# Layer 0's shared experts with plain float32 products instead of three products of split operands

## What is computed

```python
def _L0_ffn_ref(x, w_router, wg, wu, wd, sg, su, sd):      # E, TOPK, H, I, NSH = (8, 2, 256, 640, 2)
    logits = jnp.einsum('th,eh->te', xt, w_router)
    topk_w, topk_i = jax.lax.top_k(jax.nn.sigmoid(logits), TOPK)
    ...
    sgate = jax.nn.silu(jnp.einsum('th,jih->tji', xt, sg))
    sup = jnp.einsum('th,jih->tji', xt, su)
    out = out + jnp.einsum('tji,jhi->th', sgate * sup, sd)
x = x + _L0_ffn_ref(_layernorm(x), ...)
```

## Time and profile before

| | |
|---|---|
| median of 3 runs | 1225.46 us (1220.16 to 1228.32) |
| the profiled execution | 1225.15 us |
| its span, first to last instruction | 1223.4 us |
| mean granted clock of TensorE | 0.865 |
| busy: TensorE, VectorE, ScalarE, GpSimd | 965.5, 644.6, 355.5, 242.9 us |

### The profile page before, as it was taken

How to read it: one execution, slowest core, us unless ns; L and a number is a source line. 1 busy time by engine, 2 the same in 40 slices (tenths; PEclk the granted TensorE clock), 3 DMA queues, 4 the chain that set the end, 5 groups by cost and what they waited for, 6 DMA issues and landing times. The chain is left out here.

```text
span 1223.4 us, 13908 instructions
## 1 busy us (share of the span) xinstructions
PE 965.5 (79%) x4883; PEld 625.8 (51%) x4883; DVE 644.6 (53%) x1198; ACT 355.5 (29%) x747; POOL 242.9 (20%) x223
## 2 busy tenths in 40 slices
PE   3666663999998998036878888888887199999997
PEld 1333432786665665013444444444453188888885
DVE  3677675343222222464685666757743555555553
ACT  1222222232222222021523424334332043333332
POOL 0111212300000000602212203213210033344342
PEclk9778775999999999556997797899885599999999
DMA  5000002350578774330000000000000263333201
GB/s 200 1 18 18 18 1 86 100 232 5 180 286 286 274 280 153 113 114 5 3 16 18 1 18 18 1 18 14 1 1 1 91 212 121 97 114 116 94 1 34
DMA packets 36972, 102.68 MB, mean 84 GB/s; under 512 B 4640, under 2 KB 23968, under 8 KB 33712
## 3 DMA queue, kind: packets, MB, share of 16 engines
q1 hardware_dynamic: 35376, 97.70, 23.5%
q0 software_dynamic: 1536, 4.20, 1.0%
HBM read 90.54 MB, written 11.34 MB: 83 GB/s over the span
## 5 line engine op out<-in xcount | busy, mean ns | idle before, releaser
L1286 POOL TENSOR_TENSOR f_h<-f_hu,f_cb 128x512 f32<-128x512 f32 x56 | 92.9, 1659 | 173.3 <-DVE f_hu L1355 173.3
L1114 PE MATMUL ps<-f_rw,f_xT 128*128 128x512 f32 (+1 forms) x276 | 112.8, 532 | 11.2 <-DMA f_rw<-w_routed 10.6
L2028 ACT ACTIVATE b_PX<-ps 128x512 f32<-128x512 f32 x128 | 74.8, 596 | 92.3 <-PE ps L2236 91.3
L1028 DVE TENSOR_TENSOR f_rh<-f_gate,ps 128x256 f32<-128x256 f32 (+1 forms) x69 | 26.0, 377 | 135.8 <-ACT f_gate L974 85.3
L1849 DVE TENSOR_REDUCE b_smax<-ps 128x2 f32<-128x512 f32 x128 | 82.3, 685 | 28.4 <-PE ps L2216 28.2
L1355 DVE TENSOR_TENSOR f_hu<-f_act,ps 128x512 f32<-128x512 f32 x56 | 38.5, 688 | 106.9 <-PE ps L1382 106.9
L1380 PE MATMUL ps<-xh,f_wh 128*128 128x512 f32 x224 | 89.0, 398 | 5.3 <-DVE f_wl L1341 5.3
L1382 PE MATMUL ps<-xh,f_wl 128*128 128x512 f32 x224 | 89.5, 400 | 0.0
L1381 PE MATMUL ps<-xl,f_wh 128*128 128x512 f32 x224 | 89.2, 398 | 0.0
L1310 ACT ACTIVATE f_act<-ps 128x512 f32<-128x512 f32 x56 | 33.6, 601 | 145.7 <-PE ps L1382 145.7
L2236 PE MATMUL ps<-b_Q,b_Cx 100*128 100x256 f32 x256 | 71.8, 381 | 4.6 <-ACT b_Q L2020 3.6
(11 more groups left out here) (288 smaller groups left out, 1914.4 us busy)
## 6 DMA issues: line engine op xcount, KB each, us to landing
f_rw<-w_routed SPq DMA_DIRECT2D x23, 1920.0 KB, 7.9
f_raw<-w_ffn SPq DMA_DIRECT2D x28, 384.0 KB, 4.5
f_cb<-comb SPq DMA_DIRECT2D x16, 512.0 KB, 4.2
f_raw<-w_shared SPq DMA_DIRECT2D x10, 384.0 KB
b_Cx<-ctx_parts SPq DMA_DIRECT2D x96, 32.0 KB
f_cb<-comb SPq DMA_DIRECT2D x8, 384.0 KB, 3.6
rows<-a_empty SPq DMA_DIRECT2D x1, 2944.0 KB, 14.3
f_xs<-rows SPq DMA_DIRECT2D x23, 128.0 KB, 7.5
```

Of the source, the lines that this page charges most:

```text
L1114: mm = nc.tensor.matmul(ps[:, u % 4, 0:2 * n], xT[b % 2][:, c, :], rw[b % R_SLOTS][:, off:off + 2 * n], start=(c == 0), stop=(c == C - 1))
L1286: nc.gpsimd.tensor_tensor(h[u % h_slots][:], hu[u % 2][:], cb[slot][:, t * HT:(t + 1) * HT], ALU.mult).then_inc(h_ready, 1)
L2028: nc.scalar.activation(PX[g % RING][:].rearrange("p c m -> p (c m)"), ps[:, RETS + G_TURN[g] % 2, :], ACT.Exp, scale=XSC).then_inc(turn_re ...
```

## The change

The turned rows are kept once, in float32: `keep_xT` with k = 2 writes straight into a new buffer `XT` [128, 2, 1024], and `route` reads it. `high_part` and `low_part` are gone, `xh` and `xl` serve the layer 1 stages only. In the shared experts every product is one plain float32 matmul of `raw` and `XT` or `h`. The splits of weights and of `h` are gone on both engines, so are the zero products: `start` and `stop` stand on the first and last chunk's products. TensorE waits for the landing of a chunk (`w_loaded`) and for `h_ready`; a weight slot is loaded again, and an `h` slot written again, once `down` is done with it. The order of units on each engine, `LAG` and the numbers of slots stay.

```diff
@@ attention0 @@
-            def low_part(i, s):
-                t = i * 2 + s
-                dve.wait_ge(xh_ready, i * 2 + s + 1)
-                nc.vector.tensor_tensor(xl[:, :, bass.ds(t * P, P)], xT1[s][:], xh[:, :, bass.ds(t * P, P)].bitcast(F32),
-                                        ALU.subtract).then_inc(low_ready, 1)
...
-                to = xT[s] if k == 0 else xT1[s]
-                nc.scalar.copy(to[:], at.rearrange("p (c t) -> p c t", c=C)).then_inc(xT_ready[k], 1)
+                to = (xT[s][:], xT1[s][:], XT[:, :, (i * 2 + s) * P:(i * 2 + s + 1) * P])[k]
+                nc.scalar.copy(to, at.rearrange("p (c t) -> p c t", c=C)).then_inc(xT_ready[k], 1)
...
-            def high_part(i, s):
-                t = i * 2 + s
-                act.wait_ge(xT_ready[2], i * 2 + s + 1)
-                nc.scalar.copy(xh[:, :, bass.ds(t * P, P)], xT1[s][:]).then_inc(xh_ready, 1)
...
@@ routed_experts @@
                 if j >= W_SLOTS:
-                    sp.wait_ge(wh_ready, j - W_SLOTS + 1)
-                    sp.wait_ge(wl_ready, j - W_SLOTS + 1)
+                    sp.wait_ge(down_done, (j - W_SLOTS + 1) * HALVES)
...
-                if u >= 1:
-                    high_h(u - 1)
-                if u % HALVES == 0 and u // HALVES + LEAD < SHARED_CHUNKS:
-                    split(u // HALVES + LEAD)
-            high_h(UNITS - 1)
-            act.wait_ge(sum_done, 1)
+            act.wait_ge(down_done, UNITS)
...
                 if u >= H_SLOTS:
-                    dve.wait_ge(hl_ready, u - H_SLOTS + 1)
+                    dve.wait_ge(down_done, u - H_SLOTS + 1)
                 nc.vector.tensor_tensor(h[u % H_SLOTS][:], act_out[u % 2][:], ps[:, 2 * (u % 2) + 1, :], ALU.mult).then_inc(h_ready, 1)
-                if u >= 1:
-                    low_h(u - 1)
-                if u % HALVES == 1 and u // HALVES + LEAD < SHARED_CHUNKS:
-                    split(u // HALVES + LEAD)
-            low_h(UNITS - 1)
-            dve.wait_ge(sum_done, 1)
+            dve.wait_ge(down_done, UNITS)
...
                 if t == 0:
-                    pe.wait_ge(wh_ready, j + 1)
-                    pe.wait_ge(wl_ready, j + 1)
+                    pe.wait_ge(w_loaded[w], 16 * (j // W_SLOTS + 1))
...
-                        mm = three(ps[:, 2 * (u % 2) + n, :], wh[w][:, at], wl[w][:, at], xh[:, c, tok], xl[:, c, tok],
-                                   c == 0, c == C - 1)
+                        mm = nc.tensor.matmul(ps[:, 2 * (u % 2) + n, :], raw[w][:, at], XT[:, c, tok], start=(c == 0), stop=(c == C - 1))
...
-                pe.wait_ge(hh_ready, u + 1)
-                pe.wait_ge(hl_ready, u + 1)
+                pe.wait_ge(h_ready, u + 1)
...
-                    mm = three(acc[c][t], wh[w][:, at], wl[w][:, at], hh[u % H_SLOTS][:], hl[u % H_SLOTS][:], False, False,
-                               skip_group_check=True)
+                    mm = nc.tensor.matmul(acc[c][t], raw[w][:, at], h[u % H_SLOTS][:], start=(u < HALVES), stop=(u >= UNITS - HALVES),
+                                          skip_group_check=True)
...
-            pe.wait_ge(zeros_set, 1)
-            for c in range(C):
-                for t in range(HALVES):
-
-                    nc.tensor.matmul(acc[c][t], zeros[:, 0:P], zeros[:], start=True, stop=False, skip_group_check=True)
...
-            for c in range(C):
-                for t in range(HALVES):
-                    mm = nc.tensor.matmul(acc[c][t], zeros[:, 0:P], zeros[:], start=False, stop=True, skip_group_check=True)
-            mm.then_inc(sum_done, 1)
```

More of the change, by code:

```diff
@@ L99, in decoder_kernel @@
         with nc.sbuf_tensor("XN", [P, TILES, D], F32) as XN, \
+                nc.sbuf_tensor("XT", [P, C, TOKENS], F32) as XT, \
                 nc.sbuf_tensor("KR", [P, R_ALL], F32) as KR, \
@@ L526, in _ @@
                 for s in range(2):
-                    if last:
-                        low_part(i - 1, s)
-                for s in range(2):
                     if own:
@@ L744, in route @@
                 for c in range(C):
-                    mm = nc.tensor.matmul(side(s)[:, 0:E0], xT1[s][:, c, :], W[:, c, A_R:A_R + E0],
+                    mm = nc.tensor.matmul(side(s)[:, 0:E0], XT[:, c, (i * 2 + s) * P:(i * 2 + s + 1) * P], W[:, c, A_R:A_R + E0],
                                           start=(c == 0), stop=(c == C - 1))
@@ L797, in attention0, with routed_experts @@
     end_program(nc, semaphores)
-def routed_experts(nc, tag, w_shared, w_routed, rows_dram, y_dram, X, XN, xh, xl, K, ps, dest, wk, eb):
+def routed_experts(nc, tag, w_shared, w_routed, rows_dram, y_dram, X, XN, XT, K, ps, dest, wk, eb):
     ctx = ExitStack()
@@ L806, in routed_experts @@
     UNITS = HALVES * SHARED_CHUNKS
-    LEAD, LAG = 2, 2
+    LAG = 2
     W_SLOTS, H_SLOTS = 4, 4
@@ L827, in routed_experts @@
         raw = [sb(f"raw{n}", [P, WC]) for n in range(W_SLOTS)]
-        wh = [sb(f"wh{n}", [P, WC], F32R) for n in range(W_SLOTS)]
-        wl = [sb(f"wl{n}", [P, WC], F32R) for n in range(W_SLOTS)]
         act_out = [sb(f"act{n}", [P, HT]) for n in range(2)]
         h = [sb(f"h{n}", [P, HT]) for n in range(H_SLOTS)]
-        hh = [sb(f"hh{n}", [P, HT], F32R) for n in range(H_SLOTS)]
-        hl = [sb(f"hl{n}", [P, HT], F32R) for n in range(H_SLOTS)]
-        zeros = sb("zeros", [P, HT], BF16)
         oT = [[sb(f"oT{c}{t}", [P, HT]) for t in range(HALVES)] for c in range(C)]
@@ L933, in _ @@
         def _(act):
[L934 to L937, removed]
-                nc.scalar.copy(wh[j % W_SLOTS][:], raw[j % W_SLOTS][:]).then_inc(wh_ready, 1)
-            def high_h(u):
-                act.wait_ge(h_ready, u + 1)
-                if u >= H_SLOTS:
-                    act.wait_ge(down_done, u - H_SLOTS + 1)
-                nc.scalar.copy(hh[u % H_SLOTS][:], h[u % H_SLOTS][:]).then_inc(hh_ready, 1)
-            for j in range(LEAD):
-                split(j)
             for u in range(UNITS):
@@ L981, in _ @@
         def _(dve):
-            def split(j):
-                dve.wait_ge(wh_ready, j + 1)
-                nc.vector.tensor_tensor(wl[j % W_SLOTS][:], raw[j % W_SLOTS][:], wh[j % W_SLOTS][:].bitcast(F32),
-                                        ALU.subtract).then_inc(wl_ready, 1)
-            def low_h(u):
-                dve.wait_ge(hh_ready, u + 1)
-                nc.vector.tensor_tensor(hl[u % H_SLOTS][:], h[u % H_SLOTS][:], hh[u % H_SLOTS][:].bitcast(F32),
-                                        ALU.subtract).then_inc(hl_ready, 1)
-            nc.vector.memset(zeros[:], 0.0).then_inc(zeros_set, 1)
-            for j in range(LEAD):
-                split(j)
             for u in range(UNITS):
@@ L1047, in _ @@
         def _(pe):
-            def three(dst, hi, lo, rhs_hi, rhs_lo, first, last, **kw):
-                nc.tensor.matmul(dst, hi, rhs_hi, start=first, stop=False, **kw)
-                nc.tensor.matmul(dst, hi, rhs_lo, start=False, stop=False, **kw)
-                return nc.tensor.matmul(dst, lo, rhs_hi, start=False, stop=last, **kw)
             def gate_up(u):
```

15 lines of the change are left out of this document (3 added, 12 removed).

## The result

| | before | after |
|---|---|---|
| median of 12 runs | 1225.43 us (1215.22 to 1246.11) | 1237.59 us (1228.08 to 1258.44) |
| ratio after to before | | 1.0095, 95% interval 1.0055 to 1.0136 |

What follows compares the result with a forecast made beforehand. The prediction took TensorE to bound the shared experts. Their stage at +15.4 us, the entry at -2.0 and the attention stage at -0.4 summed to +13.0 us, giving 1238.5 us, range 1232 to 1245.

Steps and rivals of the forecast that it cites:

- Price of a product: Shared experts: a plain float32 product takes 0.858 us against 0.680 for three split matmuls, +21.4 us over 20 units.
- The gap: Shared experts: TensorE's hole from 224.42 to 227.66 us, with the slow matmuls behind it, disappears, -4.8 us.
- The clock at the entry: Start of the shared stage: TensorE's half clock level costs 2.4 us, before and after the change alike.
- The entry: Start of the shared experts: TensorE waits only for chunk 0's landing and starts at about 208.0 instead of 209.97, -2.0 us.
- The attention stage: Attention ahead of the shared experts: removed subtractions free GpSimd's multiply pair, casts give nothing, -0.4 us.
- The new wait on SyncE: Shared weights' reload waits for `down` of both halves; hidden by four units, 20.6 us, so no cost.
- The routed stage: Routed experts behind the shared ones: still 185 us, with their loads there in time.
- The rival of later stages: Everything from 505 us on shifts against what sets the clock, giving a gain: 1233 us; chance 0.10.
- My sign of being wrong: Among the signs that would refute the forecast: a later stage changed by more than 2 us.
- Four single paces: Shared experts' product costs four full single paces, 0.907 us, +5.9 us, 1244.4 in all; chance 0.05.
- A double record: Shared experts' product is one double record of 0.43 us, making the kernel faster, 1187 us; chance 0.03.
- The hole that stays: Shared experts: TensorE's hole stays or comes back elsewhere, +4.8 us, 1243.3 in all; chance 0.12.

Runs made afterwards that it cites:

- before_two_products: The kernel before with the second of the three split products left out (output less exact): 1195.42 us, shared stage 58.6 us.
- after_late_multiply: The changed kernel with eight extra 128x512 multiplies on VectorE ahead of unit 2's multiply: 1251.29 us in one execution, shared stage 106.3 us.
- after_two_slots: The changed kernel with two slots for the shared weights in place of four: 1250.48 us, shared stage 134.0 us.
- the third version: The changed kernel with split products again, except unit 0's gate and up; rows split while first weights load: 1218.29 us, ratio 0.9932 to before.

## Why the prediction was right, and where it was not

- **Price of a product, +21.4.** Right. 5.15 us a unit against 4.08, two records a product, 0.858 us each. It came from L1114 in the same kernel. Nothing of it is hidden, as before_two_products shows from the other side.
- **The gap, -4.8.** Wrong, and the largest miss. The arithmetic of who waits for whom was right: after_late_multiply takes a delay of 4.9 us with no loss, and the late multiply in the profile of after (225.69, 0.9 us late) costs nothing. But I took a feature of one execution for one of the kernel. It came in 2 of the 7 profiles of kernels that split. As the sum was made against the execution that had it, the -4.8 had no counterpart in the median. What made this invisible: the same execution had the least time at the half level in layer 1's attention of the three (189.5 us), and its total lay on the median.
- **The clock at the entry, 2.4.** Mis-sized by 0.6. TensorE starts earlier but the clock doesn't rise earlier by as much: 6.1 us at the half level against 4.8, so 3.0 us lost. With it the stage is 103.0 + 3.0 + 0.3 = 106.3, and the forecast said 105.6.
- **The entry, -2.0.** Right: from load to product 5.1 to 5.3 us before, 3.0 to 3.3 after. That the zero products did nothing for the clock is not shown: no run takes them away alone.
- **The attention stage, -0.4.** Wrong in size: -2.7, of which the slower start of the next stage takes back 1.3. The direct part is about the 0.4 of the working, and it is the subtractions, not the casts. The step that failed is that I stopped there: the table of stretches gave the attention a clock of 0.78, and a small shift on VectorE's side moved how long TensorE stayed at the half level.
- **The new wait on SyncE, 0.** Right; its cover is worth 24.1 us of waits, as after_two_slots shows. **The routed stage** stayed as it was: 183.5 and 184.7 us against 184.3 and 185.3.
- **The sum.** To E: 20.9 - 2.1 - 2.7 = 16.1, and the table says 16. Forecast 13.0, so 3 short. The medians are 12.2 apart, 3.9 less than the stages add up to; without that, some 1241.5 would have been due. That the total lay within 1 us of the forecast is luck. The rival of later stages, a gain of 5 us at the chance of 0.10, fits the 3.9, but the clock's scatter can give as much. My sign of being wrong, a later stage changed by more than 2 us, says little by itself: layer 1's attention was 23 us longer in after's first profile, and differs by 15 between the profiles of before.
- **The rivals.** Four single paces: no, 5.15 and not 5.44 us a unit. A double record: no. The Trainium skill (Perfetto Trace Analysis, Engine Utilization) has the output rate of low/high float32 at half; a whole product has little over a quarter in the trace, since it is two records of 0.43 us against 0.227 us for one matmul of split operands. One record by itself fits the half. The hole that stays: no, it isn't there to begin with.

What stays open is why TensorE's signals come late. It is seen at the multiply of unit 2 or 3 in 4 of the 14 profiles, by 5.5, 6.3, 0.9 and 0.7 us, each time near GpSimd's last indirect transfers, which the ten others have as well. Holding these back would tell; it wasn't tried.

## What to carry to other kernels

Before a gap in a trace goes into a sum, ask whether it is in a second execution: the rhythm of a loop repeats twenty times in one profile, a gap stands once. Where a stage is bound by TensorE, three matmuls on split operands (0.680 us) are cheaper than one float32 product (0.858), as long as the engines that split keep up, which they still do here at 2.72 us a unit; at the entry the splits can be moved to where those engines idle, as the third version does. Compare kernels of which a part runs at a changing clock by the time at the half level beside the time, or the accident of a stage that nobody touched decides.

## What was not expected of the hardware

- Eight subtractions on VectorE, which by themselves put later work back by some 0.4 us, go with a half level of TensorE's clock of 6.8 us in place of 3.4 and cost 2.7 us up to the next stage, the same to 0.1 us in every profile.
- The same subtraction takes VectorE 0.43 us alone and up to 2.12 beside GpSimd's multiply, and GpSimd's pair 3.94 us in place of 3.76.
- Layer 1's attention, the same instructions each time, took 442 to 479 us in different executions with the time at the half level (145 to 260 us).
- At the half level a float32 record takes 0.85 us against 0.43, a split one 0.427 against 0.227.
- Signals of TensorE that reach VectorE 5.5 and 6.3 us late, and ScalarE about 5, in 2 of 7 profiles of kernels that split.
